# Third phase of a 16-tile transformer kernel: the next group's head is issued amid the end of this group, its router work in the next group

## Chip, cores and metric

The kernel runs on one core of a Trainium2 chip. The metric is the device time in microseconds. Three runs of the kernel before took 1821.39, 1825.43 and 1826.34 us; the median is 1825.43 us. The profiled execution is a fourth one.

## The reference, cut to what matters

The input is `x`, 16 tiles of 128 tokens with 256 features. Four pairs of a cross-attention and a feed-forward layer are added to it in turn:

```
x = x + L0_xattn(_layernorm(x), ctx);   x = x + L0_ffn(_layernorm(x))
x = x + L1_xattn(_layernorm(x), ctx);   x = x + L1_ffn(_layernorm(x))      # 8 experts, two per token
x = x + L2_xattn(_layernorm(x), ctx, key_mask)                             # one head of 256
x = x + L2_ffn(_layernorm(x))                                              # x @ w + bias + x @ a @ b
x = x + L3_xattn(_layernorm(x), ctx)
x = x + L3_ffn(_layernorm(x))                                              # 8 experts, two per token

def _L3_xattn_ref(inputs, context_sequence, ...):
    att  = attention_head(inputs, inputs, inputs, Wk1, Wq1, Wv1, use_mask=True)
    norm = layer_norm(att + inputs, gamma, beta)
    att2 = attention_head(context_sequence, context_sequence, att, Wk2, Wq2, Wv2, use_mask=False)
    norm2 = layer_norm(att2 + norm, gamma, beta)
    h  = leaky_relu(norm2 @ W1 + b1, 0.2)
    norm3 = layer_norm(h @ W2 + b2 + norm2, gamma, beta)
    return relu(norm3)
```

The router of an expert layer takes the normalised row of a token, scores the 8 experts, picks two and gives the row a place in each of the two experts' lists.

## The kernel before

The 16 tiles are worked on in 4 groups of 4 tiles, and a group in two streams (u = 0, 1) of two tiles each. The third phase holds everything between the expert layer 1 and the expert layer 3: the results of layer 1 are added to x (`combine`), then come L2 attention, L2 feed-forward, L3 attention with its three norms, and the router of layer 3. Each engine has an instruction stream of its own, in which the work stands in the order in which `phase3` writes it (L932 on TensorE, L1239 on ScalarE, L1837 on VectorE, L2177 on GpSimd); semaphores tie the streams together. Nothing reorders an engine's stream, so an instruction that waits holds up all that stands behind it. In the traces PE is TensorE's matmul side, DVE VectorE, ACT ScalarE, POOL GpSimd, SP SyncE.

The order of one group, by the names in the code (transposes run on TensorE against `ident`; nearly every result in PSUM is copied to SBUF by ScalarE):
- `front` (L999, L1893), the head of a group: on TensorE the context is transposed (`cT`) and projected (`kk`, `v2`, the score row `tr`); on VectorE the rows of layer 1 that GpSimd gathered are added to x (`combine`, L1834 and L1897), normed into N1, and the score row is finished (L1845, `extra<-bank,products_dve,v_rows`). GpSimd adds the bias of L2 attention (L2140).
- L2 attention: `xT4`, the scores `s2` (row maxima at L1851, exponentials at L1258), `v4` for later, the transposed probabilities `p2`, the output `o2`, then add, norm, `xT5`; L2 feed-forward `f2`; norm, `xT6`.
- L3 attention: `q3`, `s3`, the values `vv`, `p3`, `q4` and `o3`, `s4`, `p4`, `o4`; two norms with gamma and beta, of which GpSimd scales the first (L2195, L2197).
- feed-forward: `nT`, `h`, `leaky`, `ff`; the add of `ff` is the `TENSOR_TENSOR work<-bank,work 128x512` at L1376; norm, relu and add to x; statistics; the output norm into XN.
- the head of the next group (`front(following)`), then the router of this group: `xT7` and the logits on TensorE, `lists` (L1709) on VectorE, the list ranks on TensorE (L698), and eight indirect DMAs on GpSimd that send XN's rows to the experts' lists (`scatter`, L2142). VectorE may not write XN again before these are through (`norm_rows_free`, L1915).
- at the start of the next group GpSimd issues the gather of the group after it (`gather`, L2151), eight indirect DMAs, ahead of all its other work.

A norm is four steps: statistics (L1382), mean and variance (L1386), variance plus epsilon (L1388), the power -1/2 on GpSimd (L2125), and the normalised rows on VectorE (L1394, or twice L1845 with gamma and beta). The three groups that have a follower run as a hardware loop of three turns on every engine; the first head and the last group are straight code. PSUM results go through a ring of six banks (0 to 5) whose order is planned at build time (`BankPlan`, L78); two more banks (6, 7) serve the expert layers' sums. The experts of layer 3 start when the last group's router has planned its tiles.

## Time and profile before

| | |
|---|---|
| three runs, median (us) | 1825.43 |
| profiled execution (us) | 1828.24, its span 1826.5 |
| mean granted TensorE clock | 0.838 of 2.4 GHz |
| busy over the span | PE 74%, DVE 44%, ACT 24%, POOL 14% |
| first s2 maximum of group 0 to last output norm of group 3 (us) | 910.49 to 1310.75 |

The span is that from the first to the last instruction. Busy shares are means over phases that differ: the two expert layers (640 to 876 us and 1344 to 1780 us) keep TensorE busy without a break, the third phase does not. In the views of instructions a row gives start, duration, engine, source line, operation and operands, and in brackets how long the engine had been idle before it and what ended that.

### The profile page before, as it was taken

What the parts mean: (1) busy time and instruction counts of PE and PEld (TensorE: products, weight loads), DVE (VectorE), ACT (ScalarE), POOL (GpSimd) and SP (SyncE); (2) the same over time, 40 slices, a digit from 0 to 9 for tenths busy, and PEclk for the clock granted to TensorE, in tenths of its full rate; (3) what the DMA queues carried; (4) which work ended last, traced back from release to release, by engine and by line L of the source; (5) the groups of instructions that cost most, each with busy time, mean ns of one, the idle gap of its engine ahead of it and who ended that gap; (6) DMA issues with size and microseconds to landing.
All of it is one profiled execution on the core that took longest, in us unless ns stands there. A gap on an engine that the chain in (4) does not pass through costs nothing.

```text
span 1826.5 us, 26133 instructions
## 1 busy us (share of the span) xinstructions
PE 1344.6 (74%) x8181; PEld 1085.0 (59%) x8181; DVE 809.6 (44%) x1978; ACT 431.3 (24%) x1096; POOL 257.9 (14%) x301
## 2 busy tenths in 40 slices
PE   5776686765553289999876675767459999999970
PEld 3444444534332288888654553555359999999970
DVE  2258788688687312212347365564621211112113
ACT  2545153252121011111231222223101111111110
POOL 2010020110100200000423424232210000000015
PEclk9887786786686699999897786879579999999995
DMA  9700010100650679888200101000068878888844
GB/s 346 252 1 1 1 57 0 43 15 23 204 190 0 215 269 302 290 276 293 89 8 12 46 9 48 0 15 9 0 248 320 319 306 311 320 320 315 306 185 124
DMA packets 101129, 278.01 MB, mean 152 GB/s; under 512 B 8640, under 2 KB 74336, under 8 KB 85856
## 3 DMA queue, kind: packets, MB, share of 16 engines
q1 hardware_dynamic: 94944, 260.73, 39.5%
q0 software_dynamic: 6144, 16.79, 2.8%
q8 instruction: 19, 0.31, 0.1%
q14 instruction: 22, 0.18, 0.0%
HBM read 222.96 MB, written 54.53 MB: 152 GB/s over the span
## 4 chain that ended last, share of the span: by engine, by line
PE 44%; issue 22%; DVE 13%; DMA 7%; POOL 6%; SPq 4%; ACT 3%; another core or an unknown queue 1%; DVEq 0%; POOLq 0%; ACTq 0%
PE bank L656 40%; DMA work<-in_moe 5%; POOL expert_rows_in L2148 2%; DVE stats L1382 1%; DVE work L1845 1%; DVE work L1376 1%; POOL rstd L2125 1%; POOL extra L2158 1%; PE bank L938 1%; DVE row_max L1438 1%; DVE extra L1595 1%; ACT norm_cols L1242 1%; DVE extra L1598 1%; POOL work L2158 1%; PE bank L897 1%
## 5 line engine op out<-in xcount | busy, mean ns | idle before, releaser
L656 PE MATMUL bank<-norm_cols,work 128*128 128x128 f32 x3744 | 466.3, 279 | 29.1 <-DMA work<-in_moe 27.5
L656 PEld LDWEIGHTS bank<-norm_cols,work 128*128 128x128 f32 x3744 | 453.5, 195 | 47.2 <-issue 30.9
L1376 DVE TENSOR_TENSOR extra<-bank,span 128x256 f32<-128x256 f32 x234 | 99.5, 425 | 526.3 <-ACT span L1215 526.3
L656 PE MATMUL bank<-work,extra 128*128 128x256 f32 x936 | 240.1, 380 | 0.0
L1215 ACT ACTIVATE span<-bank 128x256 f32<-128x256 f32 x234 | 89.9, 384 | 556.9 <-PE bank L656 556.9
L656 PEld LDWEIGHTS bank<-work,extra 128*128 128x128 f32 x936 | 160.7, 191 | 12.4
L656 PE MATMUL bank<-weights,norm_cols 128*128 128x512 f32 (+1 forms) x192 | 91.7, 629 | 8.5 <-ACT norm_cols L1242 5.7
L656 PE MATMUL bank<-work 128*128 128x256 f32 (+4 forms) x260 | 69.8, 419 | 26.2 <-ACT work L1242 10.4
L2118 POOL TENSOR_TENSOR rstd<-var_eps,neg_half 128x4 f32<-128x4 f32 x17 | 17.3, 1017 | 501.8 <-DVE var_eps L1388 501.8
L755 PE MATMUL bank<-ident,work 128*128 128x128 f32 x256 | 53.7, 369 | 36.1 <-DVE att_rows L1376 27.3
L1158 ACT ACTIVATE work<-bank,row_max 128x128 f32<-128x128 f32 x256 | 69.8, 392 | 42.2 <-DVE row_max L1438 42.1
L2125 POOL TENSOR_TENSOR rstd<-var_eps,neg_half 128x2 f32<-128x2 f32 x56 | 41.4, 740 | 225.8 <-DVE var_eps L1388 225.6
L656 PEld LDWEIGHTS bank<-work 128*128 128x128 f32 (+1 forms) x260 | 44.5, 216 | 46.4 <-issue 18.5
L755 PEld LDWEIGHTS bank<-ident,work 128*128 128x128 f32 x256 | 40.0, 188 | 52.1 <-DVE att_rows L1376 29.0
L1438 DVE TENSOR_REDUCE row_max<-bank 128x4 f32<-128x512 f32 x64 | 41.1, 684 | 61.0 <-PE bank L656 57.0
L656 PE MATMUL bank<-norm_cols,weights 128*128 128x256 f32 (+1 forms) x160 | 57.5, 515 | 14.4 <-ACT norm_cols L1242 11.2
L656 PEld LDWEIGHTS bank<-weights,norm_cols 128*128 128x128 f32 x192 | 42.3, 233 | 43.1 <-issue 31.3
L897 PE MATMUL bank<-ident,att_cols 128*128 128x128 f32 x156 | 30.6, 279 | 45.4 <-DMA att_cols<-expert_rows_in 45.4
L2153 POOL COPY slot_index_gather<-slot_index 128x8 uint32 (+1 forms) x8 | 1.6, 198 | 442.3 <-DMA expert_rows_out<-att_rows 442.3
L656 PEld LDWEIGHTS bank<-norm_cols,weights 128*128 128x128 f32 x160 | 35.8, 235 | 30.9 <-ACT norm_cols L1242 13.0
L897 PEld LDWEIGHTS bank<-ident,att_cols 128*128 128x128 f32 x156 | 22.1, 144 | 53.0 <-DMA att_cols<-expert_rows_in 45.5
L1819 DVE COPY norm_cols<-bank 128x256 f32<-128x256 f32 x78 | 33.1, 424 | 42.7 <-PE bank L897 42.7
(298 smaller groups left out, 1922.6 us busy)
## 6 DMA issues: line engine op xcount, KB each, us to landing
work<-in_moe SPq DMA_DIRECT2D x78, 1024.0 KB, 8.5
work<-in_moe SPq DMA_DIRECT2D x39, 2048.0 KB, 7.6
work<-in_moe SPq DMA_DIRECT2D x39, 512.0 KB, 6.1
expert_rows_in<-zero SPq DMA_DIRECT2D x3, 5504.0 KB, 36.0
expert_rows_out<-zero SPq DMA_DIRECT2D x3, 5504.0 KB, 33.6
att_cols<-expert_rows_in SPq DMA_DIRECT2D x78, 128.0 KB, 2.2
expert_rows_out<-att_rows SPq DMA_DIRECT2D x78, 128.0 KB, 6.3
ctx_rows<-in_ctx SPq DMA_DIRECT2D x8, 512.0 KB, 3.6
```

Of the source, the lines that this page charges most:

```text
L656: return pe.matmul(o, l, r, start=a, stop=z)
L755: last = pe.transpose(ps[:, h * P:(h + 1) * P], SC[:, w, 4 * x + h, :], ident[:, :])
L897: last = pe.transpose(ps[:, c * P:(c + 1) * P], XS[:, u, c * P:(c + 1) * P], ident[:, :])
L938: last = pe.transpose(ps[:, (c * TS + t) * P:(c * TS + t + 1) * P], rows[:, u * TS + t, c * P:(c + 1) * P], ident[:, :])
L1158: last = act.activation(SC[:, u, h, :], ps[:, (h % 4) * P:(h % 4 + 1) * P], ACT.Exp, bias=MX[:, 32 + 8 * u + h:33 + 8 * u + h])
L1215: act.activation(SG[:, b, :], ps[:, 0:256], ACT.Silu).then_inc(sem("silu_slots"), 1)
L1376: return dve.tensor_tensor(o, a, b, op)
L1438: last = dve.tensor_reduce(MX[:, at:at + 4], ps[:, :].rearrange("p (h k) -> p h k", h=4), AX, ALU.max, negate=True)
L1819: dve.tensor_copy(xsT[:, u, :, :], ps[:, 0:D].rearrange("p (c n) -> p c n", c=KC)).then_inc(bank_empty[b], 1)
L2125: pool.tensor_tensor(RS[:, part], VE[:, part], neg_half[:, part], ALU.pow).then_inc(sem(f"rstd_s{u}"), 1)
L2148: pool.indirect_dma_start(out=xs_dram, out_offset=bass.IndirectOffsetOnAxis(ap=IDXG[:, 2 * t + k:2 * t + k + 1], axis=0), in_=rows[:, t, : ...
L2158: pool.indirect_dma_start(out=YA[u][:, 2 * t + k, :], out_offset=None, in_=ys_dram, in_offset=bass.IndirectOffsetOnAxis(ap=IDXP[:, u, 2 * ...
```

## The change

It rewrites the third phase's order on all engines and touches nothing else that runs (`lists` is cut into pieces, and called whole in the first phase and for the last group).
- VectorE: `combine` of the next group stands around `leaky`, the statistics for its query rows behind (with buffers of their own, `stats_query` and so on), the query rows (into XN, where N1 was used before) between the two adds of `ff`, and the maxima of the next group's `s2` close the group. The output norm goes to the buffer NA instead of XN. The router of the group before is done in pieces inside the following group. With the two streams, the second stream's add stands ahead of the first one's rows where a power is waited for.
- TensorE: `p2` is ahead of `v4`; `xT7`, logits and ranks of the group before stand inside the group; `cT` of the next group between `p4` and `o4`, `kk` ahead of `ff`, and `v2`, `tr`, `xT4`, `s2` of the next group at the end.
- ScalarE: the same order; the score row is now an activation, and the key mask a second, bf16, row that TensorE adds to the scores.
- GpSimd: the gather stands behind the second power pair of a group, the sends of the group before behind the feed-forward bias (`n2_biased`), ahead of the powers of the group's last two norms.
- SyncE waits for the sends of a group one group later, as they are issued.
- Banks 6 and 7 take the results named SIDE. The loop is gone: the four groups are straight code.

```
-    def phase(self, keys, turns, ring=None):
+    def phase(self, keys, turns, ring=None, side=()):
...
-            if key[0] == "acc":
+            if key[0] == "acc" or key[0] in side:
                 b = ACC[self.acc % len(ACC)]
...
+    SIDE = ("cT", "kk", "v2", "tr", "v4", "vv", "lg1", "rk")
...
TensorE
                 for u in streams:
-                    turned_probs("s2", "p2", u)
-                    ready(plan, turn, ("p2", u))
+                    turned_probs("p2", u)
+                    project_rows("v4", u, W3["v4"], cT)
+                    ready(plan, turn, ("p2", u))
                     weighted("o2", u, V2)
+                if prev is not None:
+                    router_cols(prev)
...
+                if prev is not None:
+                    list_ranks(plan, turn, prev + GROUPS)
+                query4(0)
+                weighted("o3", 0, VV)
+                probs3(1)
+                query4(1)
+                scores4(0)
+                weighted("o3", 1, VV)
+                scores4(1)
                 for u in streams:
+                    ready(plan, turn, ("s4", u))
+                    turned_probs("p4", u)
+                    if following is not None:
+                        ctx_cols(following, u)
...
                 for u in streams:
+                    if following is not None:
+                        ctx_keys(u)
                     pe.wait_ge(sem(f"leaky_s{u}"), g + 1)
                     project_rows("ff", u, W3["ff"], hT3)
                 if following is not None:
-                    front(following)
-                for u in streams:
-                    turned_norm(4, "xT7", u, XN)
-                logits(plan, turn, "lg1", Wr[3])
-                list_ranks(plan, turn, g + GROUPS)
-                if following is not None:
-                    front_out()
+                    start(following)
VectorE
-                r3 = lambda t: R3[:, t, :]
+                weights(5)
                 for u in streams:
                     inverse(1, "s3", u)
                 settle()
+                divided(1, "o3", 0, r3, in3)
+                stats(0, r3, 1e-3)
+                places(4)
+                maxima(2, "s4", 0)
+                divided(1, "o3", 1, r3, in3)
+                stats(1, r3, 1e-3)
+                maxima(2, "s4", 1)
+                places(5)
                 for u in streams:
+                    apply(u, 3, r3, n1, "n1_raw")
...
+                if following is not None:
+                    combine(following, following)
+                leaky(0)
+                if following is not None:
+                    combine_second(following)
+                leaky(1)
+                if following is not None:
+                    query_stats(following)
+                add_mlp(0)
+                if following is not None:
+                    query_rows(following)
+                add_mlp(1)
+                add_out(0)
+                add_out(1)
+                if following is not None:
+                    for u in streams:
+                        maxima(0, "s2", u)
+                dve.wait_ge(sem("norm_rows_free"), g + (PRIMED + GROUPS))
+                for u in streams:
+                    apply(u, 6, xrows, lambda t: NA[:, t, :], "out_normed")
GpSimd
-            def phase3(plan, turn, g, following, front_only=False):
+            def phase3(g, following, prev):
...
+                if prev is not None:
+                    scatter(prev + GROUPS, NA)
+                if following is not None:
+                    query_power(following)
+                powers(6 * g + 5)
+                if following is not None:
+                    x_bias_streams(following, "query", following + 1, BO2)
+                powers(6 * g + 6)
```

On VectorE this is what stands behind the last head rows of a loop turn before: the head's normalised rows (into `work`), the score row (`extra`), then the router from its logits (`small`) on.

```order
L1394 TENSOR_SCALAR work<-x_stream,mean_var,rstd 128x256 x4
L133 REGISTER_ALU
L1845 ISA
L1845 SCALAR_TENSOR_TENSOR extra<-bank,products_dve,v_rows 1x512
L1707 COPY small<-bank 128x32
L1712 TENSOR_REDUCE row_max<-small 128x4
L1352 REGISTER_ALU
L1376 TENSOR_TENSOR small<-small,row_max 128x32
L1376 TENSOR_TENSOR cmpa<-small 128x256
```

And this is VectorE now from the first `leaky` of group 1 on: the second half of the next group's `combine` and its statistics stand ahead of the first add of `ff` (`work<-bank,work`), its query rows (`norm_rows`) ahead of the second.

```order
L2028 SCALAR_TENSOR_TENSOR work<-work 128x2x256
L2080 SCALAR_TENSOR_TENSOR x_stream<-extra,combine_weight_group,x_stream 128x256 x4
L2028 SCALAR_TENSOR_TENSOR work<-work 128x2x256
L1494 BN_STATS stats_query<-x_stream 128x6 x4
L1498 BN_AGGR mean_var_query<-stats_query 128x2 x4
L1500 TENSOR_SCALAR var_eps_query<-mean_var_query 128x4
L1488 TENSOR_TENSOR work<-bank,work 128x512
L1494 BN_STATS stats<-work 128x6 x2
L1498 BN_AGGR mean_var<-stats 128x2 x2
L1500 TENSOR_SCALAR var_eps<-mean_var 128x2
L2094 TENSOR_SCALAR norm_rows<-x_stream,mean_var_query,rstd_query 128x256 x4
L1488 TENSOR_TENSOR work<-bank,work 128x512
```

The router's rows are gone from this place; they stand inside the group, behind the IN3 rows, the `s3` maxima and the two `o3` statistics.

On TensorE the end of a group now reads, from the second stream's `nT` on: `nT`, `h`, then `kk` ahead of each `ff`, `v2` of both streams, the score row, `xT4` of both streams, and the scores `s2` with two mask rows each.

```order
L963 MATMUL bank<-ident,work 128x128 x4
L681 MATMUL bank<-norm_cols,weights 128x256 x4
L681 MATMUL bank<-ctx_cols,weights 128x256 x4
L681 MATMUL bank<-weights,work 128x256 x4
L681 MATMUL bank<-ctx_cols,weights 128x256 x4
L681 MATMUL bank<-weights,work 128x256 x4
L681 MATMUL bank<-weights,ctx_cols 128x256 x8
L681 MATMUL bank<-ctx_cols,products_dve 1x512 x2
L963 MATMUL bank<-ident,norm_rows 128x128 x8
L681 MATMUL bank<-extra,ones 128x256
L681 MATMUL bank<-v_rows,products_dve 128x256
L681 MATMUL bank<-k_cols,norm_cols 128x128 x4
```

Before, `xT4` and `s2` stood in the next turn, behind the logits and ranks of this one.

On GpSimd this stands now in group 1 from the feed-forward bias on: the eight sends come ahead of the query power, the powers of the last two norms, and the x bias.

```order
L2429 TENSOR_TENSOR work<-work,row_bias 128x512 x2
L2382 DMA expert_rows_in<-norm_rows_layer,slot_index_group 16512x256 x8
L2374 TENSOR_TENSOR rstd_query<-var_eps_query,neg_half 128x4
L2354 TENSOR_TENSOR rstd<-var_eps,neg_half 128x2 x2
L2369 TENSOR_TENSOR x_stream<-x_stream,row_bias 128x512 x2
L2354 TENSOR_TENSOR rstd<-var_eps,neg_half 128x2 x4
```

Before, the sends closed the turn, and the gather, also eight DMAs, opened the next one directly behind them.

## Rows read from the trace of the kernel before

**Rows 1.** Windows: stretch, us, busy PE, PEld, DVE, ACT, POOL, clock, DMA.
```profile
902.30:1001.70 99.40, 73.50 (x302) 52.74 (x302) 52.05 (x151) 24.57 (x62) 31.45 (x33) 0.81 0.05 16
1001.70:1108.90 107.20, 74.86 (x316) 53.66 (x316) 58.89 (x178) 26.27 (x65) 38.72 (x41) 0.79 0.07 24
1108.90:1217.50 108.60, 74.65 (x316) 53.63 (x316) 58.71 (x178) 26.28 (x65) 38.71 (x41) 0.77 0.06 19
1217.50:1317.00 99.50, 65.84 (x272) 47.63 (x272) 50.41 (x154) 21.03 (x56) 27.96 (x29) 0.74 0.03 11
1083.00:1104.00 21.00, 18.12 (x89) 13.50 (x87) 16.63 (x48) 5.99 (x12) 3.27 (x4) 0.99 0.07 25
1113.00:1125.00 12.00, 9.61 (x44) 7.04 (x43) 3.35 (x17) 3.55 (x9) 6.02 (x7) 0.50 0.14 55
```

**Rows 2.** Timeline, DVE: first maxima of s2 and s3, last output norm.
```profile
910.49 0.42 DVE L1851 TENSOR_REDUCE row_max<-bank 128x2 f32<-128x256 f32 x1 [7.44 <-PE bank L656]
941.09 0.42 DVE L1851 TENSOR_REDUCE row_max<-bank 128x2 f32<-128x256 f32 x1 [4.50 <-PE bank L656]
1014.13 0.42 DVE L1851 TENSOR_REDUCE row_max<-bank 128x2 f32<-128x256 f32 x1 [5.01 <-PE bank L656]
1050.01 0.42 DVE L1851 TENSOR_REDUCE row_max<-bank 128x2 f32<-128x256 f32 x1 [4.50 <-PE bank L656]
1121.25 0.43 DVE L1851 TENSOR_REDUCE row_max<-bank 128x2 f32<-128x256 f32 x1 [4.98 <-PE bank L656]
1228.89 0.42 DVE L1851 TENSOR_REDUCE row_max<-bank 128x2 f32<-128x256 f32 x1 [4.00 <-PE bank L656]
1259.12 0.42 DVE L1851 TENSOR_REDUCE row_max<-bank 128x2 f32<-128x256 f32 x1 [4.43 <-PE bank L656]
1310.01 0.74 DVE L1394 TENSOR_SCALAR norm_rows<-x_stream,mean_var,rstd 128x256 f32<-128x256 f32 x2 [0.26 <-POOL rstd L2125]
```

**Rows 3.** Timeline, group 1 to 2: from the first add of ff.
```profile
1086.03 0.69 DVE L1376 TENSOR_TENSOR work<-bank,work 128x512 f32<-128x512 f32 x1 [0.16 <-PE bank L656]
...
1098.14 0.74 DVE L1394 TENSOR_SCALAR norm_rows<-x_stream,mean_var,rstd 128x256 f32 x2
...
1100.11 1.67 DVE L1834 SCALAR_TENSOR_TENSOR x_stream<-extra,combine_weight_group,x_stream 128x256 f32 x4 [0.15 <-DVE combine_weight_group L1830]
...
1107.19 1.76 DVE L1394 TENSOR_SCALAR work<-x_stream,mean_var,rstd 128x256 f32 x2 [0.26 <-POOL rstd L2125]
...
1109.53 0.17 DVE L1707 COPY small<-bank 128x32 f32<-128x32 f32 x1
...
1112.86 0.19 PE L656 MATMUL bank<-selected,tri 128*128 128x8 bf16 x1 [8.36 <-DVE selected L1716]
...
1116.11 0.17 DVE L1756 CAST slot_index_group<-small 128x8 uint32<-128x8 f32 x1
```

**Rows 4.** Timeline: an N1 scaling on POOL, kk and the logits on PE.
```profile
1066.58 1.37 POOL L2195 TENSOR_TENSOR work<-work,row_bias 128x512 f32<-128x512 f32 x1 [1.06 <-DVE work L1394]
...
1090.94 1.89 PE L656 MATMUL bank<-weights,ctx_cols 128*128 128x256 f32 x8
...
1102.22 2.27 PE L656 MATMUL bank<-w_router,norm_cols 128*128 128x8 f32 x16 [0.69 <-ACT norm_cols L1242]
```

**Rows 5.** Timeline, starts of groups 1 and 2.
```profile
1010.00 1.08 POOL L2148 DMA_INDIRECT expert_rows_in<-norm_rows,slot_index_group  x1 [6.67 <-DVE slot_index_group L1756]
...
1018.99 0.96 POOL L2148 DMA_INDIRECT expert_rows_in<-norm_rows,slot_index_group  x1 [0.30 <-issue]
...
1024.20 0.87 ACT L1242 ACTIVATE work<-bank 128x256 f32<-128x256 f32 x2 [3.98 <-remote]
...
1124.16 5.31 PE L656 MATMUL bank<-weights,ctx_cols 128*128 128x256 f32 x16
...
1138.02 0.74 POOL L2125 TENSOR_TENSOR rstd<-var_eps,neg_half 128x2 f32<-128x2 f32 x1
```

**Rows 6.** Timeline, POOL in the second phase: the slowest send.
```profile
606.26 2.02 POOL L2148 DMA_INDIRECT expert_rows_in<-norm_rows_layer,slot_index_group  x1 [0.30 <-issue]
```

563 lines of the change are left out of this document (342 added, 221 removed).

## Prediction

> **What bounds the kernel now.** First the page: TensorE is busy 74% of the span, but nothing here touches the expert layers, where it works without a break; the change lies between them. So next the windows, one for each group of the third phase [rows 1]. A group of the middle takes 107 to 109 us. PE is busy in 75 of them, VectorE in 59, ScalarE in 26, GpSimd in 39: no engine is full. The granted clock is 0.74 to 0.81 over a group, near 2.4 GHz where PE has work without a gap (1083 to 1104 us: 0.99) and 1.2 GHz where it had waited (1113 to 1125 us: 0.50). The bound is a chain of handovers PE, ScalarE, VectorE, GpSimd with two streams to fill the gaps.
>
> Then the timeline, for marks in the chain. I take the first maxima of `s2` and of `s3` of each group and the last output norm [rows 2]. They cut a group into A (s2 to s3) and B (s3 to the next group's s2). Differences of starts: A0 30.6, B0 73.0, A1 35.9, B1 71.2, A2 and B2 together 107.6, A3 30.2, and 51.6 from 1259.12 to the end of the last norm at 1310.75. Together 400.3 us. That sum is what the change can reach.
>
> Last, the timeline of the end of group 1 [rows 3], which shows why B is long. From the first `ff` add (1086.03) the group goes through two norms to XN (1098.14, 12.1 us); the combine of the next group follows (halves of 1.67 us), its norm, the score row, then the router (1109.53 to 1116.28, 6.7 us), and only then do `xT4` and `s2` get through, at the low clock: from the ranks at 1112.86, before which PE was idle 8.36 us, to the maxima at 1121.25. The tail is 35.2 us (1086.03 to 1121.25), the part of B ahead of it 36.0 (1050.01 to 1086.03). The tail is serial since VectorE does this group's end, the next one's head and the router in a row, and PE has nothing to fill it with.
>
> **The change: the tail, groups 1 and 2.** Now VectorE has the combine and its statistics ahead of the first `ff` add, the query rows between the adds. What separates the new maxima from the `ff` add is about the same two norms, 12.1 us, beside which the next head's `xT4` and `s2` are worked off. To that come:
> - the query rows in between: four of 128x256; a pair cost 0.74 [rows 2, 3] or, beside GpSimd, 1.76 [rows 3]. Value 1.5.
> - the query power, which stands behind eight sends on GpSimd. The sends took 9.95 us (1010.00 to 1019.95), one per 1.28 [rows 5], and they start at the feed-forward bias. With `nT`, `h` and the `leaky` between the bias and the `ff` add they should be nearly through; I take 1.3 to 3 us left, value 2.
> - VectorE and GpSimd slowing each other, value 1.5 (1.76 in place of 0.74 for a row pair).
>
> New tail 12.1 + 1.5 + 2 + 1.5, about 17. Off the path go the router (6.7), the two halves of combine (3.3), the head's norm and score row, XN's rows (they now come behind the maxima), and the low-clock stretch of 8.4 us, since PE keeps `kk`, `v2` and the score row to fill the wait and so should find `xT4` at the clock of 0.99.
>
> The first part, 36.0 before, now has more in it. The `s4` maxima and the pieces of the lists are ahead of the N1 rows, so GpSimd's scaling by gamma and beta (two operations of 1.37 a stream [rows 4]) no longer starts early: 2.7, taken as 3 with the wait behind a piece. One `kk` (1.89 [rows 4]) is ahead of the first `ff` and on the path; it can be cheaper where PE waits for `leaky` anyway (bounds 0 and 3.8, both streams). First part 36 + 3 + 1.9 = 41. The lists themselves (6.7 in one go) lie in VectorE's gaps at `o3`; `cT` between `p4` and `o4` costs nothing as PE waits there for the norm's transposes; if `o4` is ready it costs its own length, about 1 us.
>
> New B1 and B2: 41 + 17.5 = 58.5, against about 72. B0 has no sends and no pieces to do: 39 + 15.5 = 54.5, against 73.0. The last group has no follower; it has the sends of group 2 and the N1 lateness: 51.6 + 2.9 + 0.5 = 55.
>
> **A.** I start from A3, 30.2. `v4` (5.31 for both streams at the low clock [rows 5]) was ahead of `p2`, whether on the path or not I judge by PE having no gap there. Now `p2` is first, and one `v4` stays between `p2` and `o2`: 1.9 by `kk`, which has the same shape. The second stream's add ahead of the first one's rows where a power is waited for gives some 1.5. The logits add 2.27 at low clock [rows 4] to PE ahead of `q3`, minus what a wait for the norm hides: 2.0 taken, with `xT7` hidden. 30.2 - 5.3 + 1.9 - 1.5 + 2.0 = 27.3. For group 0, without logits, 25. A1 and A2 were longer than A3: powers waited behind the gather (1138.02), and ScalarE stood still for 3.98 at the head of group 1 [rows 5]. The gather now stands behind the second power pair; what GpSimd has next is the `o3` power, later than the `s3` maxima (1050.01 [rows 2]) and ahead of the scaling at 1066.58 [rows 4], so eight issues of 1.28 are hidden. If they weren't, that power would come 1 to 2 us late.
>
> At 3.98 ScalarE's wait is put down to "remote", and it is the only one of three turns that shows it [rows 5]. The Trainium skill ("Runtime: NRT & Kernel Launch", "Instruction fetch mechanics") says that a taken branch can force a fetch where straight code streams on; by that, the 4.0 us goes with the loop. The row does not contradict it, but one stall in three turns is weak support, and the sum does not lean on it.
>
> **What stands behind the sends.** On GpSimd: the query power, both powers of the last norms, the x bias, four output powers. Who waits: VectorE with the query rows, behind them the second `ff` add and both norms. So a late send costs the whole group its lateness. That is the most exposed step. A send took 0.96 to 1.08 in the third phase [rows 5], but 2.02 once beside a busy VectorE [rows 6]; then eight take 8 x (2.02 + 0.30), 18.6 us in place of 10.
>
> The Trainium skill ("SBUF — State Buffer", "Who interferes with whom") speaks against this placement: while VectorE holds the shared port pair GpSimd can't write the descriptors of a DMA that it issues, so sends beside dense VectorE work stretch. The trace agrees for the one send at 2.02 against 0.96 [rows 5, 6]; it shows no case of eight such sends.
>
> **Banks, SP, rest.** Banks 6 and 7 are a ring of two for eight names; each is read by ScalarE or VectorE within a few us, and the next name to need it comes later: nothing. SyncE waits for the sends before it loads the following context, which is wanted tens of us later: nothing. The second mask row is one matmul of 128x256 a stream, below 0.3: in the rounding. The score row on ScalarE leaves VectorE's last step of the head; beside the first head it should take 2 us off ahead of 910. What follows 1310.75 (last lists, last sends, first expert) is unchanged.
>
> **Sum.** New: A 25 + 3 x 27.3 = 107; B 54.5 + 2 x 58.5 + 55 = 226.5; together 333 against 400.3: 67 less, with the 2 us of the first head 69 or 70. The profiled execution took 1828.2 (span 1826.5): 1758. The median of the runs is 2.8 lower than the profiled one, so 1756.
>
> Bounds of the unknown: the sends' remainder 0 to 8.6 us in each of two groups with a follower; `kk` 0 to 3.8 in three; the N1 lateness 0 to 5 in four; A between 24 and 31 in four. All good: some 25 lower; all bad: some 55 higher.
>
> **Rivals.**
> 1. *The sends hold the tail.* Each takes 2.3 in place of 1.28, the query power comes 8.6 us late in groups 1 and 2, the last norms' powers as late in group 3: 8.6 x 3 = 26. PE then waits, the clock falls as at 1113 us [rows 1], and `xT4` with `s2` cost their 8.4 again instead of about half: 4 x 3 = 12, less what overlaps. Time about 1756 + 30 = 1786. For: rows 6, and VectorE is dense there. Against: the sends of group 0 and 1 in rows 5 were quick. Chance 0.22. A milder kind, A not shorter at all (30.2 instead of 27 in four groups, 12 us, 1768), lies inside the forecast.
> 2. *More than forecast.* PE keeps its clock near 0.99 through `nT` and `h` and in A. PE is busy in 75 us of a group at 0.77 to 0.79; at 0.90 that would be 65. If half is on the path, 4 to 5 us a group: 1756 - 18 = 1738. Against: A's waits for softmax and norms remain. Chance 0.10.
> 3. *It doesn't do what it says*: VectorE gets full and takes the bound. VectorE's work of 59 us a group [rows 1] would have to wait on itself; between combine and the `s2` maxima it now has this group's 12.1 us, the combine (3.3), statistics and rows, some 20 us in a row (16.6 busy of 21 at 1083 before [rows 1]). With both streams serial there, B gains nothing: 1756 + 4 x 15 = about 1816, or no change. Chance 0.03 for within 0.3% (5.5 us, about what a measurement of this kernel can tell from no change), and 0.02 for a small gain.
> 4. *Slower.* Straight code for four groups in place of a loop makes the engines wait for instructions. The price of one such wait is 4.0 us, the one at 1024.20 [rows 5], if it is one. To use up 70 us takes 18 of them on the path; with 20 the time is 1756 + 80 = 1836. For: four times the code on five engines. Against: the first head and group 3 are straight code before, and A3, the shortest A of the four, shows none. Chance 0.03.
>
> Forecast 0.60. Range: 1732 to 1788, which leaves out the far end of rival 1 and rivals 3 and 4. Faster 0.94, same 0.03, slower 0.03.
>
> **What would show it.** Right: from one group's first s2 maximum to the next, some 80 to 86 us instead of 107; from the first `ff` add to the next s2 maximum about 17 instead of 35.2; the clock near 0.99 at `xT4` and `s2`; no wait of PE for ranks; the query power right behind the last send; sends at 1.3 us spacing. Rival 1: sends at 2 or more and a wait of VectorE for the query power over 5 us. Rival 4: idle times of some 4 us with no releaser on the core, on more than one engine. The forecast is wrong if the two parts of B don't come near 41 and 17.5, or if A stays at 30.

## The result and the profile after

The changed kernel takes 1757.62 us (median of four runs, 1753.16 to 1768.5), the kernel before 1825.88: a ratio of 0.964, 95% interval 0.9593 to 0.9687. The forecast was 1756. (Two of the six executions of the run with the split sends, further down, took 1904.88 and 2401.57 us at a mean clock of 0.72 and 0.55; its ratio leaves them out.) The profiled execution took 1753.16 us, 75.1 less than that of before.

The same marks as in [rows 2] cut the third phase after. First the windows of the profile after: A of group 0, then A, the first part of B and the tail of group 1 (columns as in [rows 1]).

```profile
900.71:930.12 29.41, 22.54 (x98) 17.64 (x98) 12.50 (x39) 8.22 (x19) 10.44 (x12) 0.87 0.06 18
985.65:1012.78 27.13, 21.50 (x111) 17.73 (x112) 16.18 (x52) 8.15 (x21) 9.82 (x12) 0.94 0.05 13
1012.78:1052.50 39.72, 30.54 (x146) 22.56 (x145) 26.98 (x87) 13.28 (x37) 19.71 (x20) 0.87 0.10 32
1052.50:1070.83 18.33, 12.90 (x65) 9.11 (x63) 13.92 (x38) 3.70 (x7) 9.60 (x10) 0.95 0.17 58
```

And the tail of group 1 in the kernel before.

```profile
1086.03:1121.25 35.22, 21.59 (x109) 15.84 (x109) 26.57 (x86) 8.07 (x15) 10.50 (x12) 0.75 0.06 22
```

The tail went from 35.2 us at a clock of 0.75 to 18.3 at 0.95. PE is busy for 12.9 us of it in place of 21.6: less work, since the router, `cT` and one `kk` now stand elsewhere, and `xT4` and `s2` are done at the high clock (eight passes of `s2` take 1.16 us in place of 2.08). The whole account, by differences of the marks (us):

| | before | forecast | after |
|---|---|---|---|
| A0, A1, A2, A3 | 30.6, 35.9, 35.7, 30.2 | 25, 27.3, 27.3, 27.3 | 29.4, 27.1, 27.3, 27.3 |
| B0 | 73.0 | 54.5 | 55.5 |
| B1, B2 | 71.2, 72.0 | 58.5, 58.5 | 58.1, 58.0 |
| of B1: first part, tail | 36.0, 35.2 | 41, 17.5 | 39.7, 18.3 |
| B3 | 51.6 | 55 | 53.9 |
| sum | 400.3 | 333 | 336.5 |

From one group's first `s2` maxima to the next group's it is 84.9, 85.2 and 85.3 us (80 to 86 forecast).

So 63.7 us of the 75.1 lie between the marks, 3.1 in the first head (combine to first `s2` maxima 16.8 before, 13.7 after). The combine itself came 6.65 us earlier in the profile after, behind code that does the same work; 8.2 us in all lie outside what the change does. They are luck of the two profiled executions: the one after is the fastest of its four, the one before slower than all four of its runs. The medians lie 68.3 us apart, about what the marks and the first head give (66.8).

The timeline of the tail of group 1, after: DVE's first `ff` add, the last send, the query power, the query rows, the last `s2` matmul on PE, the maxima, PE's next instruction and the next `o2` add.

```profile
1052.50 0.69 DVE L1488 TENSOR_TENSOR work<-bank,work 128x512 f32<-128x512 f32 x1
...
1055.58 0.96 POOL L2382 DMA_INDIRECT expert_rows_in<-norm_rows_layer,slot_index_group  x1 [0.30 <-issue]
...
1056.56 1.05 POOL L2374 TENSOR_TENSOR rstd_query<-var_eps_query,neg_half 128x4 f32<-128x4 f32 x1
...
1057.65 1.38 DVE L2094 TENSOR_SCALAR norm_rows<-x_stream,mean_var_query,rstd_query 128x256 f32<-128x256 f32 x4 [2.96 <-POOL rstd_query L2374]
...
1064.59 1.16 PE L681 MATMUL bank<-k_cols,norm_cols 128*128 128x128 f32 x8
...
1070.83 0.75 DVE L2034 TENSOR_REDUCE row_max<-bank 128x2 f32<-128x256 f32 x2
...
1072.23 0.66 PE L1007 MATMUL bank<-ident,work 128*128 128x128 f32 x2 [6.49 <-ACT work L1342]
...
1077.13 0.87 DVE L2028 SCALAR_TENSOR_TENSOR x_stream<-bank,row_rec,x_stream 128x256 f32<-128x256 f32 x2 [4.13 <-PE bank L681]
```

The query power starts as the last send ends, and DVE had waited 2.96 us for it. The eight sends stand 1.36 us apart on average (1.28 in [rows 5]). The logits' and ranks' wait of 8.36 us [rows 3] is gone. What the prediction had not seen: PE has both `s2` ready by 1065.8, and DVE takes the maxima at 1070.8, behind this group's second add into x. PE then stands still for 6.49 us. The tail is bound by the order of DVE's own list (the run of the early maxima tests this).

### The profile page after: what moved, and what is told of

The parts are those of the page before. It is cut to its first block, busy times and chain, and to the rows that moved or that the text cites. A ratio compares the mean times of both kernels' runs of the same rounds, so it can differ in the third digit from the quotient of the medians.

```text
span 1751.4 us, 25601 instructions
## 1 busy us (share of the span) xinstructions
PE 1310.2 (75%) x8189; PEld 1069.2 (61%) x8189; DVE 804.4 (46%) x1970; ACT 429.9 (25%) x1098; POOL 258.2 (15%) x297
## 3 DMA queue, kind: packets, MB, share of 16 engines
q1 hardware_dynamic: 94944, 260.73, 41.2%
## 4 chain that ended last, share of the span: by engine, by line
PE 43%; issue 20%; DVE 14%; POOL 8%; DMA 7%; SPq 5%; ACT 2%; DVEq 0%; POOLq 0%; ACTq 0%
PE bank L681 40%; DMA work<-in_moe 5%; POOL expert_rows_in L2382 3%; DVE work L2028 2%; DVE stats L1494 1%; DVE work L1488 1%; POOL extra L2392 1%; DVE row_max L1550 1%; DVE extra L1707 1%; DVE extra L1710 1%; POOL work L2392 1%; SPq L568 1%; DVE x_stream L2028 1%; PE bank L922 1%; DMA expert_rows_in<-norm_rows_layer,slot_index_group 1%
## 5 line engine op out<-in xcount | busy, mean ns | idle before, releaser
L681 PEld LDWEIGHTS bank<-norm_cols,work 128*128 128x128 f32 x3744 | 451.3, 194 | 45.6 <-issue 29.4
L681 PE MATMUL bank<-weights,norm_cols 128*128 128x512 f32 (+1 forms) x192 | 85.1, 589 | 8.3 <-ACT norm_cols L1326 5.5
L681 PE MATMUL bank<-work 128*128 128x256 f32 (+4 forms) x260 | 67.9, 405 | 28.2 <-ACT work L1326 12.9
L780 PE MATMUL bank<-ident,work 128*128 128x128 f32 x256 | 52.3, 362 | 36.1 <-DVE att_rows L1488 27.1
L2382 POOL DMA_INDIRECT expert_rows_in<-norm_rows_layer,slot_index_group x64 | 68.6, 1071 | 59.3 <-DVE slot_index_group L1928 41.3
L1550 DVE TENSOR_REDUCE row_max<-bank 128x4 f32<-128x512 f32 x64 | 41.1, 683 | 60.4 <-PE bank L681 60.4
L681 PE MATMUL bank<-norm_cols,weights 128*128 128x256 f32 (+1 forms) x160 | 57.1, 511 | 15.3 <-ACT norm_cols L1326 12.1
L922 PE MATMUL bank<-ident,att_cols 128*128 128x128 f32 x156 | 30.6, 279 | 45.1 <-DMA att_cols<-expert_rows_in 45.1
L681 PEld LDWEIGHTS bank<-weights,norm_cols 128*128 128x128 f32 x192 | 38.4, 212 | 40.9 <-issue 27.9
L2354 POOL TENSOR_TENSOR rstd<-var_eps,neg_half 128x2 f32<-128x2 f32 x48 | 35.6, 741 | 162.8 <-DVE var_eps L1500 162.4
L681 PEld LDWEIGHTS bank<-norm_cols,weights 128*128 128x128 f32 x160 | 35.3, 232 | 31.3 <-ACT norm_cols L1326 16.7
```

Of the source, the lines that this page charges most:

```text
L681: return pe.matmul(o, l, r, start=a, stop=z)
L780: last = pe.transpose(ps[:, h * P:(h + 1) * P], SC[:, w, 4 * x + h, :], ident[:, :])
L922: last = pe.transpose(ps[:, c * P:(c + 1) * P], XS[:, u, c * P:(c + 1) * P], ident[:, :])
L1550: last = dve.tensor_reduce(MX[:, at:at + 4], ps[:, :].rearrange("p (h k) -> p h k", h=4), AX, ALU.max, negate=True)
L2354: pool.tensor_tensor(RS[:, part], VE[:, part], neg_half[:, part], ALU.pow).then_inc(sem(f"rstd_s{u}"), 1)
L2382: pool.indirect_dma_start(out=xs_dram, out_offset=bass.IndirectOffsetOnAxis(ap=IDXG[:, 2 * t + k:2 * t + k + 1], axis=0), in_=rows[:, t, : ...
```

## The experiments

Twelve kernels ran in three batches of four, each batch on one chip of its own, with the kernel before beside it. Times are compared within a batch; between batches only the ratios to the kernel before are. "Tail", "A" and "first part" are those of the table, from each kernel's profile.

**The changed kernel again** (no edit).

> The changed kernel itself, once more, as the measure for the other three kernels that run beside it. Both theories: a ratio to the kernel before of 0.964 again (0.959 to 0.969), about 1758 us; the marks of the third phase within 1 us of the first profile (first s2 maxima 85.0, 85.2, 85.3 us apart).

Ratio 0.9632 (0.9612 to 0.9653), 1759.26 us. A1 27.1, first part 39.7, tail 18.3: the marks repeat. A0 took 31.8 at a clock of 0.78 in place of 29.4 at 0.87. The combine of group 0 starts at 893.2, beside 893.7 in the kernel before. Over all fourteen profiles it starts between 885.9 and 895.8, though the code ahead of it does the same work in all: the 6.65 us are such a difference between executions.

**The head behind this group's end.**

```diff
-                    combine(following, following)
                 leaky(0)
-                    combine_second(following)
                 leaky(1)
-                    query_stats(following)
                 add_mlp(0)
-                    query_rows(following)
                 add_mlp(1)
                 add_out(0)
                 add_out(1)
...
+                    combine(following, following)
+                    combine_second(following)
+                    query_stats(following)
+                    query_rows(following)
                     maxima(0, "s2", u)
```

> The changed kernel, but on VectorE the whole head of the next group (combine, its statistics, the query rows) stands behind the output norm, as before the change, and on GpSimd the query power behind the last powers; the router stays inside the next group. Theory 1 (the tail was a series, and what counts is that the next head's chain runs beside this group's last two norms): each of three tails gets the combine 3.3, statistics and power 3, rows 1.4 and xT4 to s2 some 7 us back, less the 3 us wait for the query power: 12 to 15 us a group, 36 to 45 us, time 1794 to 1803. Rival (VectorE's sum of work is the bound of the tail, and it is the router that had to go): only the latency from rows to maxima comes back, 5 to 7 us a group, 15 to 21 us, time 1773 to 1779.

Ratio 0.9855 (0.9827 to 0.9884), 1800.47 us: 41.2 us more than the changed kernel beside it. Windows of its group 0 tail and of the A behind it, then PE at the head.

```profile
975.86:1004.69 28.83, 14.05 (x56) 9.73 (x55) 19.88 (x58) 3.91 (x7) 6.77 (x7) 0.73 0.00 0
1004.69:1034.45 29.76, 25.50 (x122) 20.76 (x122) 15.21 (x47) 8.26 (x21) 10.29 (x12) 0.86 0.07 19
```

```profile
998.76 1.12 PE L963 MATMUL bank<-ident,norm_rows 128*128 128x128 f32 x4 [14.30 <-DVE norm_rows L2094]
...
1004.69 0.42 DVE L2034 TENSOR_REDUCE row_max<-bank 128x2 f32<-128x256 f32 x1 [4.39 <-PE bank L681]
```

Tails are 28.8, in place of 15.4, 18.3 and 18.2: 34.5 us. A1 to A3 give the rest, 6.6 us more than beside it: PE comes out of a wait of 14.3 us, its clock is at 0.86 in A1. Theory 1 holds at its middle; the rival (15 to 21 us) does not. Some 60% of the gain (41.2 of 66.1 us in this batch) is the place of the head.

**The loop alone**, in the kernel before.

```diff
-            with pe.Fori(0, GROUPS - 1) as g:
+            for g in range(GROUPS - 1):
                 phase3(j3, g, g, g + 1)
```

(The same on the three other engines.)

> The kernel before, only its loop of three turns of the third phase written out straight on TensorE, ScalarE, VectorE and GpSimd. Theory 1: the loop had a small part; the 4.0 us ScalarE wait with releaser 'remote' at the head of one turn may go, 0 to 5 us in all: 1821 to 1826 us. Rival (loop turns cost every engine a start-up, and straight code is a main part of the gain): 10 us or more less, under 1816. Third (straight code makes engines wait for instructions): above 1830.

Ratio 0.9976 (0.996 to 0.9992), 1820.71 us: 4.6 us less. Its tails are 33.8 in place of 34.2 to 35.3. So the loop held a small part, and straight code alone costs nothing there. ScalarE's wait of 3.98 us [rows 5] is absent from its profile, and yet A1 takes 36.6 us (35.9 before): that wait did not make A1 long, as the prediction had supposed in part.

**Both v4 ahead of both p2.**

```diff
+                for u in streams:
+                    project_rows("v4", u, W3["v4"], cT)
                 for u in streams:
                     turned_probs("p2", u)
-                    project_rows("v4", u, W3["v4"], cT)
```

> The changed kernel with both v4 ahead of both p2 again, as before the change. Theory 1, by the prediction's term for A (5.3 in place of 1.9 on the path): A (s2 to s3 maxima) longer by 1.9 to 3.4 us in each of four groups, 8 to 14 us, time 1766 to 1772. Rival: TensorE waits 3.2 to 6.5 us for the exponentials ahead of p2 in the profile of the changed kernel, so that both v4 (3.8 us) lie in that wait and keep the clock up: A the same or shorter by up to 2 us a group, time 1750 to 1758.

Ratio 0.9638 (0.9615 to 0.9662), 1758.15 us: no difference from 0.9632. Windows of A0 to A3:

```profile
899.59:931.79 32.20, 23.94 (x98) 18.44 (x98) 12.50 (x39) 8.22 (x19) 10.43 (x12) 0.83 0.06 17
987.35:1012.72 25.37, 18.21 (x103) 14.64 (x102) 16.08 (x52) 7.81 (x21) 9.82 (x12) 1.00 0.05 15
1070.99:1099.19 28.20, 21.32 (x96) 16.63 (x96) 16.17 (x52) 7.92 (x21) 10.98 (x13) 0.82 0.06 19
1157.17:1183.81 26.64, 19.40 (x95) 15.29 (x96) 16.18 (x53) 7.81 (x21) 5.99 (x7) 0.87 0.00 1
```

For groups 1 to 3 the rival holds: both `s2` are ready early, and `v4` lies in the wait for the exponentials. For group 0 theory 1 does. There the second `s2` comes 3.2 us behind the first, and nothing fills a wait. The time from the first `s2` maxima to the first `o2` add shows both:

| first maxima to first `o2` add (us) | group 0 | 1 | 2 | 3 |
|---|---|---|---|---|
| before | 9.8 | 12.3 | 10.2 | 9.3 |
| changed (first profile) | 6.8 | 6.2 | 6.3 | 6.3 |
| both `v4` ahead | 9.3 | 4.5 | 5.5 | 5.5 |

So the equal ratio is a loss in one group against small gains in three. (In group 0 the form with `p2` first takes 6.6 to 8.2 us in the other profiles, by the clock that `v4` runs at.) A as a whole also goes with the clock: 25.4 us at 1.00, 28.2 at 0.82.

**Five sends ahead of the query power, three behind the next powers.**

```diff
-                    scatter(prev + GROUPS, NA)
+                    scatter(prev + GROUPS, NA, slice(0, 5))
                     query_power(following)
                 powers(6 * g + 5)
+                    scatter(prev + GROUPS, NA, slice(5, 8))
```

> The changed kernel, but only five of the eight sends stand ahead of the query power; three come behind the first powers of the last two norms. Theory 1 (the sends hold the query power, and with it VectorE, 2.9 us in groups 1 and 2): that wait goes, the tail (first ff add to next s2 maxima, 18.3 us) is 2 to 3 us shorter in two groups, 4 to 6 us, about 1752 to 1754. Rival (VectorE's work sets the tail and the wait only moves to the powers behind the other sends): 0 to 1 us a group, the wait appears ahead of the gamma and beta rows; 1756 to 1760.

The query rows of group 1, no wait ahead of them:

```profile
1060.79 1.38 DVE L2094 TENSOR_SCALAR norm_rows<-x_stream,mean_var_query,rstd_query 128x256 f32<-128x256 f32 x4
```

The tails of groups 1 to 3 are 16.2, 16.2 and 13.8 in place of 18.3, 18.2 and 16.1: 2.1 us in each, as theory 1 says. The ratio is 0.9653 (0.9632 to 0.9675), no gain over the changed kernel on other chips (0.9632, and 0.966 in the next batch). The first parts of this profile are 43.0 (at 0.76) and 41.2 where they were 39.7; the changed kernel, too, has 41.2 in a later profile (last section). A gain in time is not shown.

**The s2 maxima ahead of the second add into x.**

```diff
                 add_out(0)
-                add_out(1)
                 if following is not None:
                     for u in streams:
                         maxima(0, "s2", u)
+                add_out(1)
```

> The changed kernel, but VectorE takes the next group's s2 maxima ahead of the second stream's add_out and not behind it. In the profile of the changed kernel TensorE has the first s2 ready at 1064 us, the maxima are taken at 1070.8, and TensorE then waits 6.5 us for the exponentials. Theory (the tail is bound by VectorE's own order, not by the head's chain of the query rows): the next group starts 4 to 5 us earlier, and add_out lies in the 4 us wait for o2; 3 to 4 us gained in each of three groups, 9 to 12 us, about 1747. Rival: what is taken from the tail comes back in A, as VectorE does the same work ahead of the o2 add: 0 to 1 us a group, 1755 to 1758.

Ratio 0.9594 (0.9577 to 0.9611), 1757.12 us beside 1829.02 before. The three others of its batch have 0.9653, 0.967 and 0.9667, with intervals that begin at 0.963 or above: it is the fastest form, by 0.4 to 0.7% against the changed kernel (0.9632 and 0.966, other chips) and by 0.6 to 0.8% against its neighbours. Windows of the tail of group 1 and of A2 behind it, then PE in A1:

```profile
1068.19:1081.02 12.83, 12.49 (x62) 8.86 (x61) 10.64 (x26) 3.71 (x7) 7.53 (x7) 1.00 0.23 73
1081.02:1110.41 29.39, 22.90 (x117) 18.82 (x117) 19.91 (x62) 8.04 (x21) 10.60 (x13) 0.88 0.04 12
```

```profile
1006.56 1.06 PE L963 MATMUL bank<-ident,norm_rows 128*128 128x128 f32 x4 [3.93 <-DVE norm_rows L1506]
...
1008.31 3.78 PE L681 MATMUL bank<-weights,norm_cols 128*128 128x256 f32 x8 [0.69 <-ACT norm_cols L1326]
```

The tails are 11.7, 12.8 and 12.0: 3.7 to 6.2 us less than in the changed kernel, 15.4 in all. Part comes back in A: PE now waits 3.93 us for the first norm (1.06 in the changed kernel), since DVE does its add into x and the output rows ahead of the `o2` add, and comes out of it at the low clock (3.78 us for eight passes that take 1.99 at the high one). A1 to A3 are 30.7, 29.4 and 30.2, the first parts of groups 1 and 2 43.3 and 43.0, so that the marks of this profile add up to 340.1 us, no less than in the changed kernel (336.5, 339.3 and 343.6). The profiled execution is this kernel's slowest (1765.47): that the tails shrink is shown by its rows, that something is left of it by the times alone. Both readings had something; by the ratios the gain is 7 to 12 us.

**Query rows behind both ff adds.**

```diff
                 add_mlp(0)
-                    query_rows(following)
                 add_mlp(1)
+                    query_rows(following)
```

> The changed kernel, but the query rows stand behind both adds of ff instead of between them. Theory: in groups 1 and 2 the second add and its statistics (2 us) fill the wait of 2.9 us for the query power, 2 us gained in each; in group 0, without sends, nothing: 3 to 4 us, about 1754. Rival: the later rows put off xT4 and s2 and TensorE becomes late: no gain, 1758 or more.

Ratio 0.967 (0.9651 to 0.9689): the rival. The tails of groups 1 and 2 fall to 16.7 and 16.5, that of group 0 grows from 15.4 to 16.6, and with it nothing is left: first part and tail of group 1 are 58.0 us together, as in the changed kernel (58.1).

**Both kk behind both ff.**

```diff
-                        ctx_keys(u)
                     pe.wait_ge(sem(f"leaky_s{u}"), g + 1)
                     project_rows("ff", u, W3["ff"], hT3)
+                if following is not None:
+                    for u in streams:
+                        ctx_keys(u)
```

> The changed kernel with both kk behind both ff. Theory by the prediction's term (1.9 us of kk on the path ahead of the first ff, in three groups): 3 to 6 us gained, about 1753. Rival: ff waits for leaky anyway, which stands behind half of the combine on VectorE, and kk only fills that wait: no difference within 2 us, or up to 5 us lost through a lower clock.

Ratio 0.9667 (0.9651 to 0.9683): no gain. Its first parts are 39.8, 41.1 and 41.5, as in the changed kernel's third profile (39.8, 41.2, 41.5), its tails 15.3, 18.3 and 18.2. But the rival's reason, that `ff` waits for `leaky`, isn't what the rows show. The first `ff` add of group 1 follows VectorE's statistics for the query rows without a wait (first row); with the head behind, where these are gone and `kk` is still ahead of `ff`, the same add waits for PE (second row, from that run).

```profile
1058.11 0.69 DVE L1488 TENSOR_TENSOR work<-bank,work 128x512 f32<-128x512 f32 x1
```

```profile
1074.10 0.69 DVE L1488 TENSOR_TENSOR work<-bank,work 128x512 f32<-128x512 f32 x1 [1.97 <-PE bank L681]
```

`kk` on PE, and half a combine with the statistics on VectorE, are two chains of one length side by side. Taking either away alone gains nothing; both away was not run.

**The changed kernel, third time** (third batch, another chip).

> The changed kernel once more, as the measure for the kernels that run beside it: a ratio to the kernel before of 0.963 (0.960 to 0.966).

Ratio 0.966 (0.9633 to 0.9687), 1764.73 us, its tails 15.3, 18.3, 18.2 as ever. What is longer is told in the last section.

**Extra matmuls in PE's waits.**

```diff
+                def warm(name, u, count):
+                    ps, b = fill(plan, turn, (name, u))
+                    for n in range(count):
+                        mm(ps[:, 0:D], ident[:, :], W3["v4"][:, 0, :])
...
+                    idle = {(0, 0): 3, (2, 0): 16}
+                    if prev is None:
+                        idle = {(0, 0): 4, (1, 0): 7, (2, 0): 16}
...
+                    warm("p2", u, 12 if u == 0 and prev is not None else 0)
...
+                    if u == 0:
+                        warm("o4", u, 7)
```

(The keys of `idle` name the transposes: (0, 0) is the first `xT5`, (1, 0) the first `xT6`, (2, 0) the first `nT`.)

> The changed kernel with extra matmuls of 128x256 on TensorE (ident by a weight, into a bank that is overwritten directly after; they take no part in the result) where it waits: 12 ahead of the first p2 of groups 1 to 3 (wait 3.2 to 6.5 us), 3 or 4 ahead of the first xT5, 7 ahead of the first xT6 of group 0, 7 ahead of the first o4 (wait 2.2), 16 ahead of the first nT (wait 4.4). Theory (what is left of the spread in the third phase is the clock: A takes 25.4 at a granted 1.00, 27.1 at 0.94, 30.5 at 0.78, and the part ahead of the ff adds 39.7 at 0.87 and 43 at 0.80): the clock is near 1.0 in all of them, A 25.5 to 27, the first part 36 to 38, in all 12 to 20 us less, ratio 0.953 to 0.957. Rival (the chain is latency of ScalarE, VectorE and GpSimd, and the clock falls over the whole kernel as its budget is used elsewhere): the clock does not rise or the stages do not shrink, ratio 0.962 to 0.966, or more where the extra matmuls stand in the way.

Ratio 0.9667 (0.9646 to 0.9689), 1767.7 us: no gain, though the clock over the span rose from 0.852 to 0.876. The windows of the first part of B0, and the extra work ahead of `nT` in group 1:

```profile
936.03:975.11 39.08, 36.45 (x178) 28.34 (x178) 24.73 (x70) 13.17 (x36) 13.97 (x14) 1.00 0.10 31
```

```profile
1041.89 7.07 PE L681 MATMUL bank<-weights,ident 128*128 128x256 f32 x32
```

The dose was wrong: each of these matmuls is two passes, so that 16 take 7.07 us in a wait of 4.4, and 12 take 5.34 ahead of `p2`. The place was wrong too, in group 2: there the work waited as long as `p2` itself would have, and then stood in the way at the low clock. A2 is 32.6 us for it.

```profile
1079.74 7.37 PE L681 MATMUL bank<-weights,ident 128*128 128x256 f32 x24 [6.97 <-ACT work L1355]
```

At 1.00 the first parts are 39.1 to 41.4 us, as long as at 0.87 without the extra work, with some 2.6 us of it too much ahead of `nT` alone. What a right dose gives was not run.

**Early maxima with extra matmuls.** The edits of both, with 14 matmuls ahead of the first `xT5` and none ahead of `p2`.

> The s2 maxima ahead of the second stream's add_out, together with the extra matmuls that take no part in the result: 14 ahead of the first xT5 (where TensorE waited 3.9 us with the early maxima), 7 ahead of the first o4, 16 ahead of the first nT, none ahead of p2. Theory: B 3 to 4 us shorter than in the changed kernel as with the early maxima alone, and A at 27 to 28 and not at 29 to 31, since the clock no longer falls in the wait; ratio 0.945 to 0.953. Rival: A stays near 30, since VectorE does add_out and the output rows ahead of the o2 add: ratio 0.957 to 0.961, as with the early maxima alone.

Ratio 0.965 (0.9632 to 0.9668): what the early maxima had is gone. The tails are 11.4, 14.4 and 14.3, but A1 to A3 are 31.7 to 33.0 at clocks of 0.90 to 0.95: 14 extra matmuls take 6.2 us there, in a wait of 3.9.

**The gather ahead of a group's powers.**

```diff
+                    gather(following, g + 1)
                 powers(6 * g + 1)
                 x_bias_streams(g, "normed", 3 * g + 1, BF2)
                 powers(6 * g + 2)
-                    gather(following, g + 1)
```

> The changed kernel with the gather at the start of a group's work on GpSimd, ahead of its first powers, as before the change. By the prediction (the powers waited behind the gather in A1 and A2; the move takes 2 to 4 us off each): GpSimd is busy with it until some 11 us after the last output power, A1 and A2 2 to 4 us longer than 27.2, A0 unchanged or up to 4 us longer, time 1762 to 1768. Rival: the first power is not wanted before the gather is through: nothing, 1756 to 1760.

Ratio 0.9706 (0.9683 to 0.9729), 1772.93 us, 8.2 us more than the changed kernel beside it. The first power of group 1 follows the last issue of the gather without a gap, and VectorE waits for it:

```profile
1000.29 0.95 POOL L2392 DMA_INDIRECT extra<-expert_rows_out,slot_index_gather  x1 [0.30 <-issue]
...
1001.25 0.75 POOL L2354 TENSOR_TENSOR rstd<-var_eps,neg_half 128x2 f32<-128x2 f32 x1
...
1002.04 0.74 DVE L1506 TENSOR_SCALAR norm_rows<-x_stream,mean_var,rstd 128x256 f32<-128x256 f32 x2 [2.76 <-POOL rstd L2354]
```

A1 and A2 are 32.3 and 31.7, 2.4 and 3.2 more than in the changed kernel of the same batch (29.8, 28.5), A0 the same. Beside that kernel the stretches are as predicted; the time is not (1762 to 1768 expected), and what the 8.2 us hold beyond these 5.6 isn't known.

## Why the prediction was right, point by point

- **The tail** (17.5 forecast, 18.3 measured; without sends 15.5 and 15.4). The head beside this group's end takes it off the path: undone, it costs 34.5 us in tails and 41 in all. The terms too: 2.96 us of wait for the query power (1.3 to 3 forecast), which the split sends take away with 2.1 us of the tail. But the series was not the one described, and the terms listed add up to 17.1, not to the 17.5 that the sum uses. The next head's chain is through 5 us early; the tail ends when DVE's list lets the maxima come. Moving only them takes 3.7 to 6.2 us off it.
- **The first part** (41, measured 39.7). The term of 3 us for the later N1 scaling and the pieces of the lists was too large. Group 3 has both but no `kk` or combine ahead of its `ff`, and takes 37.8. Group 1 before took 36.0, with the second `h` at the same high clock. So they cost 1.8 us (no run isolates them). Groups 0, 2 and 3 before took 37.7 to 37.9 because the second `h` ran at the low clock there (3.60 us in group 3 in place of 1.99); in the straight form of that kernel two groups have the fast `h` and take 36.1, two the slow one and take 37.8 and 38.0. The other 1.9 us of groups 1 and 2 have the size of the term for `kk`, but `kk` alone does not hold them, as the run with `kk` behind `ff` and the one with the head behind show. (The row called `kk` in [rows 4] is one of `v2`; `kk` itself took 1.99.)
- **A of groups 1 to 3** (27.3, measured 27.1 to 27.3) is right in its value, not in its account. What shortened A3 from 30.2 shows at the first `o2` add of group 3, before (with `v4`, the second maxima and `p2` ahead of it) and after.

```profile
1231.80 4.41 PE L656 MATMUL bank<-weights,ctx_cols 128*128 128x256 f32 x16
...
1232.05 0.42 DVE L1851 TENSOR_REDUCE row_max<-bank 128x2 f32<-128x256 f32 x1 [2.73 <-issue]
...
1236.05 0.38 PE L982 MATMUL bank<-ident,work 128*128 128x128 f32 x2
...
1238.17 0.88 DVE L1845 SCALAR_TENSOR_TENSOR x_stream<-bank,row_rec,x_stream 128x256 f32<-128x256 f32 x2 [0.82 <-PE bank L656]
```

```profile
1162.41 0.88 DVE L2028 SCALAR_TENSOR_TENSOR x_stream<-bank,row_rec,x_stream 128x256 f32<-128x256 f32 x2 [4.13 <-PE bank L681]
```

From first maxima to that add it was 9.28 us before and is 6.31 now; from there to the `s3` maxima 20.95 and 20.96. Before, PE goes from the late second `s2` (its maxima, at 1232.05, 3.2 us behind the first [rows 2]; the row names no releaser, the three like it name PE) through both `v4` to `p2` without a gap, so `v4` was on the path, as the prediction had judged. Two parts of the change each take it off. With `p2` first it is 6.8 in group 0, where the second `s2` is still late. With both `s2` ready it is 5.5 even with `v4` first. Priced at 3.4 us in four groups, the order of `p2` and `v4` is worth up to 3 in group 0, and nothing in the others, where the tail's surplus does it. The terms for the adds (1.5 less) and the logits (2.0 more) together come to nothing in 20.95 and 20.96; no run takes them apart.
- **A0** (25, measured 29.4) is the term that failed outright. The prediction took 2 us off for the missing logits and 1.5 for the new order of the adds. Its first piece did shrink as said (9.8 to 6.8), but from the `o2` add to the `s3` maxima it grew, from 20.8 to 22.6. Timeline of A0: the second stream's add, PE's `xT6` and the matmuls behind it, then the same matmuls in A1:

```profile
919.30 0.69 DVE L1488 TENSOR_TENSOR x_stream<-x_stream,bank 128x512 f32<-128x512 f32 x1 [1.42 <-PE bank L681]
...
920.93 0.66 PE L963 MATMUL bank<-ident,work 128*128 128x128 f32 x4 [1.74 <-DVE work L1506]
...
922.27 3.64 PE L681 MATMUL bank<-norm_cols,weights 128*128 128x256 f32 x8 [0.69 <-ACT norm_cols L1326]
...
1006.58 1.99 PE L681 MATMUL bank<-norm_cols,weights 128*128 128x256 f32 x8 [0.69 <-ACT norm_cols L1326]
```

VectorE now waits for PE with the add that stands ahead of the first stream's rows. So `xT6` comes late (PE waits 1.74 us; 0.21 before the change), and PE comes out of the wait at the low clock, which costs 1.65 us. In A1 the logits stand in that place, and the row runs at the high clock. That makes the router's work in A free (20.96 us with it, 20.95 in A3 before without it). It does not show that it gains time: in the old order this piece takes no longer without it. Seven extra matmuls in that wait of A0 (the run with extra matmuls) bring the row back to 1.99 us but start it later, and this piece takes 22.0 us beside 22.6.
- **The gather**: the prediction gave it no price of its own; 2 to 4 us for each of A1 and A2 were expected of the run that puts it back, and it costs 2.4 and 3.2. The sends stood directly ahead of it before; no run puts both back.
- **The sends beside a busy VectorE.** They stand 1.36, 1.35 and 1.31 us apart in groups 1 to 3, in place of 1.28; one of the eight in group 1 took 1.47 in place of 0.96. What the Trainium skill states in "SBUF — State Buffer", "Who interferes with whom" (GpSimd can't write a DMA's descriptors while VectorE holds the ports that they share), shows at most in that one send; rival 1 is out.
- **The loop.** 4.6 us by itself, with or without the cause that the Trainium skill gives ("Runtime: NRT & Kernel Launch", "Instruction fetch mechanics"). No run tells which.
- **Rival 4** (straight code makes engines wait): up to ten waits without a releaser on the core, 0.2 to 3.3 us each, in some executions; see below. The kernel before has such waits too, so they don't tell against straight code. What is there is small.

The errors cancelled in part. `v4` was priced at 3.4 in four groups and is worth it in one at most, the N1 scaling at 3 and costs 1.8, and A0 was off by 4.4. Against that stand both `s2` being ready and the second `h` at the high clock, which were not seen. That the total came within 2 us of the measured median (1756 and 1757.62) is luck in this part; that the gain comes from the tails is not. The sum between the marks was off by 3.5 us of 64.

## What to carry to other kernels

Where one engine's list serves two chains, ask at which place of that list the next chain's result is taken, not only when it is ready: here moving two row maxima by one norm was worth more than any of the other orders tried. Work of one stage put into the waits of another is cheaper than its length: here the router's work in A cost nothing. And a term of a sum is only shown by the run that undoes it, read group by group: one order cost 2.5 us in one group and gave back 0.8 to 1.6 in each of the others, with no difference in the total. Where two chains of one length stand side by side, undoing one shows nothing; `kk` and the combine had to be read together.

## What the runs showed of the hardware that was not expected

- **The clock differs from execution to execution in the same code.** A0 is the same in the changed kernel and in five of its variants. In their eight profiles it took 29.1 to 29.6 us at a granted 0.86 or 0.87 (four times), 31.6 and 31.8 at 0.78 and 33.4 at 0.72 (twice): 4 us in one stretch of 30. The windows of A0 in the run of the early maxima, which does not touch it:

```profile
909.40:942.78 33.38, 26.90 (x98) 20.54 (x98) 12.59 (x39) 8.22 (x19) 10.42 (x12) 0.72 0.05 16
```

- **Waits with a releaser "remote" come and go with the run.** The third phase has none in the first two profiles of the changed kernel, seven in the third profile:

```profile
939.53 0.42 DVE L2034 TENSOR_REDUCE row_max<-bank 128x2 f32<-128x256 f32 x1 [3.19 <-remote]
...
939.99 0.37 ACT L1342 ACTIVATE work<-bank,row_max 128x128 f32<-128x128 f32 x1 [2.81 <-remote]
...
1111.41 0.42 DVE L2034 TENSOR_REDUCE row_max<-bank 128x2 f32<-128x256 f32 x1 [2.18 <-remote]
```

PE had ended the `s3` that DVE waited for here at 936.9. All seven other profiles of the second and third batch show them too (on two chips), mostly at the `s3` maxima on DVE and the `vv` copies on ScalarE, with ten in one of them; in the first batch, on another chip, four profiles show none. With them the first parts of groups 1 and 2 are 41.2 and 41.5 in place of 39.7, and the phase from combine to last output norm is 357.2 us in the third profile of the changed kernel, 350.2 and 352.3 in the others. They are not a matter of this change: one of them stands in the first phase, which it doesn't touch, in the profile of the kernel before and, within 0.1 us of the same length, in all eight of the second and third batch, and in none of the other five.

```profile
477.29 0.20 ACT L1184 ACTIVATE router_logits<-bank 128x32 f32 x1 [6.73 <-remote]
```

Whether the chip, the place of the code in memory or something else decides it stays open, and so does what this one costs: without it the combine of group 0 starts at 885.9 to 893.2, with it at 888.9 to 895.8.
- **A higher mean clock came without less time.** Over the span it rose from 0.852 to 0.876 with the extra matmuls, and the time was the same, within 0.2%. These matmuls stood in the way in part (A2 32.6 us), so the run does not show what the clock is worth by itself.
